# Start of a LoRA feed-forward kernel: row numbers first on GpSimd, LoRA-B gathered before the second half of x, all of LoRA-A on SyncE

## What is computed

```python
def lora_add(base, inp, A, B):
    Ab = A[layer_idx][lora_indices]          # one adapter of rank 16 for each of the 8 sequences
    Bb = B[layer_idx][lora_indices]
    t = jnp.einsum('bri,bni->bnr', Ab, inp)
    return base + jnp.einsum('bor,bnr->bno', Bb, t) * SCALE
gate = lora_add(jnp.einsum('bnh,fh->bnf', x, W_gate), x, A_gate, B_gate)
up = lora_add(jnp.einsum('bnh,fh->bnf', x, W_up), x, A_up, B_up)
act = jax.nn.silu(gate) * up
down = lora_add(jnp.einsum('bnf,hf->bnh', act, W_down), act, A_down, B_down)
```

## Time and profile before

| what | value |
|---|---|
| three timed executions | 363.3, 362.2, 363.18 us; median 363.18 |
| the profiled execution | 365.2 us, its span 363.5 us |
| TensorE busy | 356.8 us, 98% of the span |
| VectorE, ScalarE, GpSimd busy | 198.0, 141.6, 89.5 us |
| mean granted TensorE clock | 0.995 of full |

### The profile page before, as it was taken

One profiled execution on the slowest core, in us unless ns is written; L12 is line 12 of the kernel. 1 busy time (PEld: TensorE's weight loads), 2 busy tenths in 40 slices (PEclk: granted clock), 3 DMA queues, 4 the chain that ended last, 5 costly groups with the idle time before them and its releaser, 6 DMA issues.

```text
span 363.5 us, 4759 instructions
## 1 busy us (share of the span) xinstructions
PE 356.8 (98%) x1728; PEld 301.0 (83%) x1728; DVE 198.0 (54%) x302; ACT 141.6 (39%) x192; POOL 89.5 (25%) x95
## 2 busy tenths in 40 slices
PE   8997999999999999999999999999999999999997
PEld 7786888888888888998888898888888888888886
DVE  1838645554355434466565567579978877511101
ACT  3637641434144323345474354539343353201100
POOL 3757778545430000300000000000023065002200
PEclk9998999999999999999999999999999999999999
DMA  7934453321320014639524406401033012201011
GB/s 255 288 138 145 110 160 105 98 87 58 115 96 19 0 28 147 202 126 386 183 60 169 134 2 257 206 0 58 2 111 122 2 58 58 60 29 58 31 58 58
DMA packets 14914, 38.86 MB, mean 107 GB/s; under 512 B 2368, under 2 KB 4160, under 8 KB 13616
## 3 DMA queue, kind: packets, MB, share of 16 engines
q1 hardware_dynamic: 11584, 30.75, 24.8%
q0 software_dynamic: 2880, 7.48, 7.0%
q10 hardware_dynamic: 432, 0.39, 0.3%
HBM read 36.51 MB, written 2.10 MB: 106 GB/s over the span
## 4 chain that ended last, share of the span: by engine, by line
PE 91%; DMA 3%; POOL 2%; ACT 1%; issue 1%; DVE 1%; POOLq 0%; SPq 0%
PE ps L1030 28%; PE ps L1031 28%; PE ps L1032 27%; PE ps L1050 3%; PE ps L1152 3%; DMA b_raw<-b_gu,row_of 2%; POOL b_raw L376 1%; PE ps L1242 1%; DMA small_sb<-small_in 1%; PE ps L1229 1%; ACT t_st L432 1%; ACT b_st L432 1%; DVE b_st L699 1%; PE ps L1251 0%; POOLq L364 0%
## 5 line engine op out<-in xcount | busy, mean ns | idle before, releaser
L1030 PE MATMUL ps<-x_hl,w_hl 128*128 128x512 f32 x160 | 63.2, 395 | 0.0
L1031 PE MATMUL ps<-x_hl,w_hl 128*128 128x512 f32 x160 | 63.2, 395 | 0.0
L1032 PE MATMUL ps<-x_hl,w_hl 128*128 128x512 f32 x160 | 62.6, 391 | 0.0
L376 POOL DMA_INDIRECT b_raw<-b_gu,row_of x44 | 45.1, 1026 | 35.0 <-DVE b_st L699 22.8
L415 POOL TENSOR_TENSOR am_hl<-am_raw,am_hl 128x512 fp32r<-128x512 f32 x8 | 11.2, 1405 | 136.7 <-ACT am_hl L432 136.7
L720 DVE TENSOR_TENSOR glu<-glu,ps 128x512 f32<-128x512 f32 x22 | 15.0, 684 | 39.4 <-PE ps L1050 39.4
L1032 PEld LDWEIGHTS ps<-x_hl,w_hl 128*128 128x128 f32 x160 | 30.3, 190 | 6.7
L432 ACT ACTIVATE act<-glu 128x512 f32 (+1 forms) x22 | 13.8, 631 | 55.0 <-DVE glu L720 51.7
L1030 PEld LDWEIGHTS ps<-x_hl,w_hl 128*128 128x128 f32 x160 | 30.4, 190 | 5.4
L1031 PEld LDWEIGHTS ps<-x_hl,w_hl 128*128 128x128 f32 x160 | 30.5, 191 | 4.9
L1030 PE MATMUL ps<-act,wd_hl 128*128 128x512 f32 x80 | 31.1, 389 | 0.0
(11 more groups left out here) (136 smaller groups left out, 700.3 us busy)
## 6 DMA issues: line engine op xcount, KB each, us to landing
wc_raw<-mask_w SPq DMA_DIRECT2D x8, 1024.0 KB, 7.2
w_raw<-w_gu SPq DMA_DIRECT2D x9, 512.0 KB
wd_raw<-w_dn SPq DMA_DIRECT2D x10, 256.0 KB
x_raw<-x_t SPq DMA_DIRECT2D x8, 256.0 KB, 6.7
w_raw<-w_t SPq DMA_DIRECT2D x2, 1024.0 KB, 7.3
x<-x_t SPq DMA_DIRECT2D x2, 1024.0 KB, 6.3
am_raw<-a_moe SPq DMA_DIRECT2D x8, 256.0 KB, 2.6
bm_raw<-b_moe SPq DMA_DIRECT2D x4, 512.0 KB, 3.8
```

Source lines behind the costliest of these rows:

```text
L376: nc.gpsimd.indirect_dma_start(b_raw[f % 2][:, p].rearrange("q m f -> q (m f)"), None, b_gu, bass.IndirectOffsetOnAxis(ap=row_of[:, f, p:p ...
L1030: nc.tensor.matmul(out, w_high, m_high, start=start, stop=False)
L1031: nc.tensor.matmul(out, w_high, m_low, start=False, stop=False)
L1032: return nc.tensor.matmul(out, w_low, m_high, start=False, stop=stop)
```

## The change

GpSimd no longer starts with the two loads of W (blocks 2 and 3 of tiles 0 and 1). It loads the small table itself, works out the row numbers, waits until the first block of x is there, then issues the two loads of W and the gathers. SyncE issues the loads of x's first half and of W block 1, then all eight loads of LoRA-A (before: five, GpSimd three), and only then the second half of x and the constants. The loads of W for tiles 2 and 3 wait until LoRA-B of tiles 0 and 1 has landed. ScalarE's copies of W block 0 move to VectorE, and the LoRA-A copies and subtractions come ahead of the whole second half of x.

```diff
-A_BY_SP = 5
@@ sync
             load_x0(0)
-            sp.dma_start(small_sb[:], small_in).then_inc(dma_small, 16)
             load_x0(1)
             for u in range(2):
                 sp.dma_start(w_raw[u][:, 1], w_gu[u, :, 1]).then_inc(dma_w_first[u][1], 16)
             for k in range(2, KD):
                 load_x0(k)
-            for k in range(KD):
-                sp.dma_start(x_raw[:, k, HALF:T], x_t[:, k, HALF:T]).then_inc(dma_x1[k], 16)
             sp.wait_ge(dma_small, 16)
-            for b in range(A_BY_SP):
+            for b in range(BATCH):
                 adapter = sp.value_load(itok_all[0:1, b:b + 1], min_val=0, max_val=ADAPTERS - 1)
                 sp.dma_start(a_raw[:, b].rearrange("q k m r -> q (k m r)"),
                              a_gu[bass.ds(adapter, 1)]).then_inc(dma_a, 16)
+            for k in range(KD):
+                sp.dma_start(x_raw[:, k, HALF:T], x_t[:, k, HALF:T]).then_inc(dma_x1[k], 16)
             sp.dma_start(const_sb[:], consts).then_inc(dma_const, 16)
             def load_tile(f, slot):
+                sp.wait_ge(dma_b[slot], 64)
                 for made in (w_hi, w_lo):
@@ gpsimd
-            for u in range(2):
-                pool.dma_start(w_raw[u][:, 2:KD], w_gu[u, :, 2:KD]).then_inc(dma_w_first[u][2], 16)
-
+            pool.dma_start(small_sb[:], small_in).then_inc(dma_small, 16)
             pool.wait_ge(dma_small, 16)
-            for b in range(A_BY_SP, BATCH):
-                adapter = pool.value_load(itok_all[0:1, b:b + 1], min_val=0, max_val=ADAPTERS - 1)
-                pool.dma_start(a_raw[:, b].rearrange("q k m r -> q (k m r)"),
-                               a_gu[bass.ds(adapter, 1)]).then_inc(dma_a_pool, 16)
             nc.gpsimd.tensor_scalar(itok_first[:], itok_own, RANK, None, ALU.mult).then_inc(row_step, 1)
             pool.wait_ge(row_step, 1)
             nc.gpsimd.tensor_tensor(row_of[:], row_sb, ...
             pool.wait_ge(row_step, 2)
+            pool.wait_ge(dma_x0[0], 16)
+            for u in range(2):
+                pool.dma_start(w_raw[u][:, 2:KD], w_gu[u, :, 2:KD]).then_inc(dma_w_first[u][2], 16)
@@ scalar
-            for k in range(2):
-                x_high(k, 0)
-                for u in range(2):
-                    w_first_high(u, slice(k, k + 1), k)
+            x_high(0, 0)
+            x_high(1, 0)
+            act_e.wait_ge(w_hi, 2)
+            for u in range(2):
+                w_first_high(u, slice(1, 2), 1)
             x_high(2, 0)
             for u in range(2):
                 w_first_high(u, slice(2, KD), 2)
             x_high(3, 0)
-            for k in range(2):
-                x_high(k, 1)
-            act_e.wait_ge(dma_a, 16 * A_BY_SP)
-            act_e.wait_ge(dma_a_pool, 16 * (BATCH - A_BY_SP))
+            act_e.wait_ge(dma_a, 16 * BATCH)
             for m in range(2):
                 for par in range(2):
                     copy(a_part(a_st, m, 0, par), a_own(m, par)).then_inc(a_hi, 1)
-            for k in range(2, KD):
+            for k in range(KD):
                 x_high(k, 1)
@@ vector
+            for u in range(2):
+                dve.wait_ge(dma_w_first[u][0], 16)
+                nc.vector.tensor_copy(w_hl[u][:, 0, 0:1], w_raw[u][:, 0:1]).then_inc(w_hi, 1)
             for k in range(2):
                 x_low(k, 0)
...
             x_low(3, 0)
-            for k in range(2):
-                x_low(k, 1)
             for m in range(2):
                 for par in range(2):
                     dve.wait_ge(a_hi, 2 * m + par + 1)
                     low(a_part(a_st, m, 1, par), a_own(m, par), a_part(a_st, m, 0, par)).then_inc(a_lo, 1)
-            for k in range(2, KD):
+            for k in range(KD):
                 x_low(k, 1)
```

More of the change, by code:

```diff
@@ L192, in build @@
         dma_b = [sem(f"dma_b{u}") for u in range(2)]
-        dma_a, dma_a_pool, dma_ad = sem("dma_a"), sem("dma_a_pool"), sem("dma_ad")
+        dma_a, dma_ad = sem("dma_a"), sem("dma_ad")
         dma_wd = [sem(f"dma_wd{u}") for u in range(2)]
```

## The result

The changed kernel takes 365.19 us (median of 14; 363.99 to 367.57) against 362.37 (median of 14) for the kernel before: ratio 1.0066, 95% interval 1.0045 to 1.0088. The medians lie 2.8 us apart; the ratio is an estimate of its own and not the quotient of the two medians, and stands for 2.4 us, its interval for 1.6 to 3.2. By either the change costs time. The forecast was 2.4 us of gain. Two executions of versions further down, one of 443.9 us and one of 694.3 us at a mean clock of 0.755 and 0.911, are in no median and no ratio.

What follows compares the result with a forecast made beforehand. TensorE, busy 98% of the span, was taken as the bound, so only its holes and clock could give time. Gains of 0.77 (fourth group) and 1.63 (dip) made 2.4 us: 363.18 to 360.8, 8 in 10 within 359.0 to 363.0.

Steps and rivals of the forecast that it cites:

- A new wait at LoRA-A: TensorE, ready at 16.98 us, would wait 1.6 us for LoRA-A from SyncE's eight serial loads and start about 18.6.
- x's second half and not the gathers ahead of b_high(0): On ACT, the high part of tile 0's LoRA-B would follow the x copies, starting at 21.0 instead of 21.77 us.
- W of blocks 2 and 3 without a wait: Issued later, behind the table, these loads might hold TensorE up to 1.7 us, covered by the LoRA-A wait; taken as nothing.
- hole at 9 us: TensorE's 0.81 us gap waiting for block 1 of x and W would close, as 512 KB no longer compete.
- the hole at 6.7: W block 0's copies on VectorE would move the first x_low by up to 0.4 us; cost taken as nothing.
- the subtraction at the end: Final step: summed gain 2.4 us taken from the profiled 365.2, then from the median 363.18, giving 360.8 us.
- dip: Granted clock falling to 0.50 near 31 us at TensorE's second LoRA-B stall; forecast gone, gaining 1.63 us.
- fourth group: TensorE's four adaptation matmuls of tile 1 would start at 29.37 instead of 30.14 us, gaining 0.77.
- the landing terms: Assumed arrivals: the table at 5.03 us, 3.6 after issue, and x's second half at about 20.5 us.
- The second rival: The clock falls all the same, at the second stall (362.4 us) or the LoRA-A stall (361.4); chance 0.22.
- the third: Rival: x's second half lands late, at 22.9 us, b_high(0) starts at 23.5, time 364.9; chance 0.08.
- No cost: Holding W of tiles 2 and 3 costs nothing: tile 2's lands near 24 us, ACT wants it at 28.

Runs made afterwards that it cites:

- second profile of the kernel before: The kernel before, unedited, timed and profiled once more: median 361.83 us, ratio 0.9987; profiled execution 361.69 us, without a clock dip.
- the table by SyncE: The changed kernel with the small table loaded by SyncE as its second DMA again: 365.31 us, ratio 1.0067 against the kernel before.
- the late x: The kernel before with x's second half issued behind its five LoRA-A loads and LoRA-A first on ACT and DVE: 363.63 us, ratio 1.0052.
- the hold: The kernel before with only W of tiles 2 and 3 held until LoRA-B of tiles 0 and 1 has landed: 360.54 us, ratio 0.9942.
- x first: The changed kernel with SyncE's four loads of x's second half ahead of LoRA-A again: 362.07 us, ratio 0.9997 against the kernel before.
- SP alone: The kernel before with all eight LoRA-A loads by SyncE, behind x's second half, none by GpSimd: 364.39 us, ratio 1.0054.

## Why the prediction was wrong

**The order of the chain was right.** A new wait at LoRA-A, released by DVE's LoRA-A parts, of 1.74 us where 1.6 was forecast; x's second half and not the gathers ahead of b_high(0); 8.35 us from there to TensorE (22.78 to 31.13) where 8.37 was forecast; W of blocks 2 and 3 without a wait; no hole at 9 us. Two of these need a word. The wait at LoRA-A has the length of the forecast because both its ends came about 0.5 us late: TensorE was there at 17.4 and not 16.98, held by the hole at 6.7 that the forecast had put at 0.4 at worst, and started at 19.16 and not 18.6. And the hole at 9 us was not in the second profile of the kernel before either, so its absence after the change doesn't show that the change closed it.

**The step that failed is the subtraction at the end**: "it lay 2.0 above the median, so the median is 363.18 - 2.4 = 360.8". Most of the 2.4 was the way back from what made that one execution slow. Its 1.63 for the clock was a dip that 68 of 76 executions of the kernel before do not have, and its b_high(0) at 21.77 was 1.9 late by the second profile. Slowness of the profile was taken off twice, once as the distance to the median and once as the gain. From profile to profile the change did gain, 365.2 - 364.59 = 0.6 us, which is the dip won back (1.63) less a fourth group 0.99 later; but few executions of the kernel before had that to give (8 of 76 a dip). The three times of 362.2 to 363.3 beside the 365.2 would have told: priced against a base 2.0 us better, 0.77 + 1.63 is a gain of 0.4 at most, and the landing terms below make it a loss. Against the second profile even the forecast's own fourth group, 29.37, is 1.1 us later than the 28.26 of the kernel before. The error of 365.19 - 360.8 = 4.4 us is made of this 2.0, 1.8 in the profiled execution (364.59 against the forecast 362.8), and 0.6 by which the changed kernel's median lies above its own profile, which had no dip.

**The 1.8 us are the sizes of two landings.** The table took 4.92 us and not 3.63, so LoRA-A's issues began at 7.28 and not 5.97; the pace was 1.10 and not 1.14, the last went at 15.01, not 13.95, and ACT took LoRA-A 2.1 later, at 17.14, not 16.64. The last of the four x loads was issued at 16.96, not 16.2, and took 5.26 us to land instead of about 4.3: 22.24 instead of about 20.5, inside the bounds of 3.6 and 6.7 but on the far side. b_high(0) came 1.8 after the forecast's 21.0. The Trainium skill, page "DMA: Bandwidth & Descriptors", in its section on the anatomy of one DMA, gives 2.0 us plus bytes over 436 GB/s, an estimate of 2.1 us for the table by GpSimd. These runs do not agree: in four profiles with GpSimd as the issuer of the table it took 4.3 to 4.9, and the measurement decides. By SyncE it took 3.4 to 4.0 in the eight others.

**The dip** was forecast gone. It is more frequent: 6 of 14 against 8 of 76 of the kernel before. The second rival had named the risk, with 0.22 and a far smaller cost, because I believed a dip to be the rule before. Which of the two waits of the changed kernel brings it no profile shows, as the profiled execution had none; with the table by SyncE it lay behind the second.

**The rivals.** The nearest was the third, x's second half late, 0.08, which put the landing from which it decides at 21.2 us: the landing was 22.2. From the profile of the earlier trace rows that is 1.0 us lost with the dip won back; from the second profile it is the whole 2.87 us.

**The parts together.** Alone, the late x costs 0.52% and LoRA-A by SyncE 0.54%, and the hold gains 0.58%, each within 0.2 to 0.25: in sum 0.48%, against 0.66% for the whole. That they nearly add up says little, as dips are mixed into them. By the medians without a dip they cost 1.3 and 0.7 us and gain 1.5, in sum 0.5 us, against 2.2 to 2.4 for the whole. The parts work on each other: x behind eight loads lands later than behind five, and with x last the hold has nothing to give. LoRA-A by SyncE, the hold and what else is in the change, without the late x, make 0.9997. The hold, which I forecast at nothing, is the one of the three that pays. "No cost" was right, but in the earlier trace rows the 6.29 us between last gather and landing was a transfer in a crowd, and the step asked what the hold delays, not what W's 1 MB had been delaying.

What stays open: why the dip comes in one execution and not in the next with waits of the same length, the worth of the table's issuer, which lies under it, why the gathers took 6.29 us in one profile of the kernel before and 4.47 in the other, and what the copies of W block 0 on DVE and the new order on GpSimd are worth alone, which no run tests.

## What to carry to other kernels

- Hold the profiled execution against the timed ones before pricing: if it is slower than their range, find what in it is not usual (a clock dip, a late landing) and take that out of the base; a gain made of removing it is none.
- When several loads go to one queue, those that need no register should be issued while the queue waits for the one that does: four plain loads moved from behind eight dependent ones to ahead of that wait gave back 2.5 to 3.1 us here, although they made TensorE wait 0.9 us for W.
- If a transfer that all wait for lands late, look for the big one issued beside it that nobody needs yet, and hold that one: here one wait cut the time from last gather to use from 4.8 to 3.0 us and brought 1.5 us (2.1 by the ratio), the largest gain of any version here, 360.54 us. Where something else is last, the same wait brings nothing.
- The worth of one part measured alone is not its worth beside the others: without a dip, the late x cost 1.3 us behind five loads (363.35 against 362.04) and 2.3 behind eight (364.4 against 362.07 with x first).

## What the runs showed of the hardware

- The last of four gathers of 128 KB is in ACT's hands 3.0 us after its issue with the DMAs at a share of 0.3 from 16 to 20 us, 3.7 with 1 MB of x beside it (share 0.85 from 16 to 18 us), 4.8 and 6.3 in the two profiles with 1 MB of W beside it, and 6.6 with 1 MB of x and 1 MB of W.
- The table of 32 KB took 4.3 to 4.9 us to land as GpSimd's first DMA (four profiles) and 3.4 to 4.0 as SyncE's second (eight profiles), in each case beside the first loads of x and W.
- From one LoRA-A load, whose address is first read from the table, to the next SyncE takes 1.14 us in the profile before, 1.10 in the one after and up to 1.28 in the others; for a plain load of x's second half, 0.62 before and 0.46 after.
- A wait of the same 1.7 us on TensorE came with and without a fall of the granted clock. Behind the 1.73 of the changed kernel's profile the clock stays at full rate, 2.4 GHz; behind the 1.72 of the version with the table by SyncE it is at 0.50, 1.2 GHz. The windows of the first and of the second:

```profile
32.00:33.00 1.00, 1.00 (x6) 0.82 (x5) 1.00 (x3) 0.48 (x2) 0.95 (x1) 1.00 0.31 94
```

```profile
32.00:33.00 1.00, 1.00 (x4) 0.80 (x3) 1.00 (x2) 0.97 (x2) 0.69 (x2) 0.50 0.57 86
```

Behind the 2.48 us of SP alone, too, it stays at full rate in the profile, though ten of its twelve executions had a dip.
